# Moving the next weights' transposes, the segment sums and the leaf lookups within one block of a Mamba-style mixer, and multiplying the B C product by dt on VectorE

## The reference

```
proj = h @ in_proj_w.T            # gate z, then x B C, then dt
xBC  = silu(causal_conv4(xBC))    # 4 taps along the 32 tokens
dt   = softplus(dt + dt_bias);  dA = exp(dt * A)
state = state * dA + dt * x * B;  y = state . C      # 32 steps
y = y + x * D;  y = group_rmsnorm(y) * norm_weight * silu(z)
x = x + y @ out_proj_w
```

## Time and profile before

| | us |
|---|---|
| median of 3 runs (lowest, highest) | 3438.72 (3436.22, 3439.60) |
| the profiled execution: its time / its span | 3441.43 / 3439.3 |
| busy in the span: PE, DVE, ACT, POOL | 3311.1, 2740.2, 1746.8, 716.8 |
| granted TensorE clock, share of full speed | 0.996 |
| one iteration, groups 0 to 6 | 47.7 |
| stage 2, from its first to its last inverse root on POOL | 161 to 3160 |

### The profile page before, as it was taken

The page is one execution under the profiler, slowest core; times in us unless marked ns, Lnnn a source line. Parts: engine busy times, 40 slices in busy tenths (PEclk is TensorE's granted clock), DMA queues, the critical chain, the costliest instruction groups (busy, mean ns, idle before and its releaser), DMA issues. The chain is left out here.

```text
span 3439.3 us, 86265 instructions
## 1 busy us (share of the span) xinstructions
PE 3311.1 (96%) x33306; PEld 2741.3 (80%) x33306; DVE 2740.2 (80%) x4367; ACT 1746.8 (51%) x3203; POOL 716.8 (21%) x520
## 2 busy tenths in 40 slices
PE   8999999999999999999999999999999999999999
PEld 6777877778777787777877778777787777787888
DVE  6788888888888888888888888888888878887443
ACT  5666665555455554555555555545555555554111
POOL 1122212122221222112221122211122112221333
PEclk9999999999999999999999999999999999999999
DMA  7432363334533353335433262334423342224331
GB/s 267 168 120 106 113 232 123 116 122 161 168 124 114 125 192 134 128 110 184 133 134 133 105 220 98 134 132 176 149 98 134 140 166 98 73 98 152 93 91 58
DMA packets 207792, 466.28 MB, mean 136 GB/s; under 512 B 35134, under 2 KB 80606, under 8 KB 198284
## 3 DMA queue, kind: packets, MB, share of 16 engines
q1 hardware_dynamic: 206364, 464.72, 38.9%
q0 software_dynamic: 368, 0.85, 0.1%
q10 hardware_dynamic: 1024, 0.27, 0.0%
HBM read 313.68 MB, written 152.09 MB: 135 GB/s over the span
## 5 line engine op out<-in xcount | busy, mean ns | idle before, releaser
L1155 PE MATMUL low_banks<-ht,wt 128*128 128x512 f32 x6912 | 1612.8, 391 | 0.8 <-DVE xc L1383 0.8
L1155 PEld LDWEIGHTS low_banks<-ht,wt 128*128 128x128 f32 x6912 | 1292.4, 188 | 274.8 <-DVE xc L1383 1.2
L1383 DVE SCALAR_TENSOR_TENSOR xc<-low_banks,cvw,xc 128x496 f32<-128x496 f32 (+2 forms) x1152 | 824.9, 717 | 102.3 <-ACT xc L1287 65.9
L1243 PE MATMUL bank<-wot,gy 128*128 128x512 f32 x3072 | 733.6, 394 | 96.2 <-DVE gy L1432 96.2
L1243 PEld LDWEIGHTS bank<-wot,gy 128*128 128x128 f32 x3072 | 567.1, 188 | 236.6 <-DVE gy L1432 122.3
L1287 ACT ACTIVATE xc<-low_banks,cvb,cvw 128x512 f32<-128x512 f32 x384 | 299.8, 781 | 698.7 <-PE low_banks L1155 698.7
L1092 POOL TENSOR_TENSOR r<-rv,neg_half 128x4 f32<-128x4 f32 x64 | 64.5, 1008 | 1569.1 <-DVE rv L1465 1569.1
L1277 ACT ACTIVATE gy<-z 128x512 fp32r<-128x512 f32 x256 | 161.7, 632 | 311.1 <-DVE z L1449 311.1
L1073 POOL TENSOR_TENSOR segr<-adts,mask_le 128x1024 fp32r<-128x1024 f32 x128 | 242.8, 1918 | 336.7 <-DVE adts L1374 336.7
L1087 POOL TENSOR_TENSOR y<-y,step_of 128x512 f32<-128x512 f32 x128 | 174.8, 1389 | 627.1 <-ACT y L1293 627.1
L1473 DVE SCALAR_TENSOR_TENSOR acc<-bank,r,acc 128x512 f32<-128x512 f32 x256 | 176.7, 745 | 86.7 <-PE bank L1243 69.3
(11 more groups left out here) (195 smaller groups left out, 3726.3 us busy)
## 6 DMA issues: line engine op xcount, KB each, us to landing
ht<-h_d SPq DMA_DIRECT2D x63, 2048.0 KB, 8.6
acc_d<-acc SPq DMA_DIRECT2D x64, 1024.0 KB, 4.3
wt_d<-wnext SPq DMA_DIRECT2D x112, 512.0 KB, 3.6
acc<-acc_d SPq DMA_DIRECT2D x56, 1024.0 KB, 7.0
wt<-wt_d SPq DMA_DIRECT2D x70, 512.0 KB, 7.7
stage<-in_L_attn_in_proj_w SPq DMA_DIRECT2D x84, 256.0 KB, 2.7
wot<-wt_d SPq DMA_DIRECT2D x28, 512.0 KB, 6.3
xb<-in_x SPq DMA_DIRECT2D x8, 1024.0 KB, 7.7
```

The lines of the kernel that those rows point to most:

```text
L1155: ins = pe.matmul(pb[:, :], wt[:, n, l, k, :], ht[:, rr, k, :], start=(q == 0 and k == 0), stop=(q == 2 and k == KC - 1))
L1243: ins = pe.matmul(bank[OUT[t]][:, :], gy[:, c, l, t * P:(t + 1) * P], wot[:, rr, c, :], start=(c == 0 and q == 0), stop=(c == CT - 1 and q ...
L1383: ins = dve.scalar_tensor_tensor(dst, src, cvw[:, n, TAPS - 1 - k:TAPS - k], dst, ALU.mult, ALU.add)
```

## The change

1. **PE.** The segment sums move from behind chunk 5 and the B C products to behind chunk 3. The B C products move behind chunk 7. The transposes of the next weights move from before the scan to between the scan and chunk 9. The output projection no longer waits for both low halves at its start: its bank order becomes (7, 5, 6, 4), and ahead of banks 5 and 6 it waits for the first and the second low half.
2. **ACT.** The two `Exp` come before the tap of chunk 4. The high halves of the next weights come behind all four `skip`, one before `high(0)`, one behind it; the squares become operations of their own.
3. **DVE.** The four `pair` and `find_here` move behind the last convolution chunk. `m` is made in other steps: `joint`, the B C products spread over the heads times `step_of` (one of 128x1024), then `joint` times `decay` (two of 128x512). The last joins move behind the sums of squares; the low halves of the next weights move between the steps of the gated output.
4. **POOL.** `decay_products` is gone.

The core of the diff:

```diff
-    XT, SEG, CB, OUT, SSQ, NEXT = (4, 5, 6, 7), (4, 5), 3, (5, 6, 7, 4), 3, (5, 6)
+    XT, SEG, CB, OUT, SSQ, NEXT = (4, 5, 6, 7), (4, 5), 3, (7, 5, 6, 4), 3, (5, 6)
...
-        def decay_products(g, j):
...
-                pool.tensor_tensor(decay[:, tiles, :, :], decay[:, tiles, :, :], step_of[:, tiles, :, :], ALU.mult).then_inc(s_stepped, 1)
...
                 project(n)
+                if n == NCV - 3:
+                    sum_segments()
+
+            for c in range(CT - 2):
+                pe.wait_ge(s_conv, NCV * it + 4 + c)
+                project(NCV + c)
...
-            for u in range(2 if prepare else 0):
-                pe.wait_ge(s_raw[u], 16 * it + 16)
-                pe.wait_ge(s_dtx, TT * it + 2 + u)
-                for k in range(KC):
-                    ins = pe.transpose(bank[NEXT[u]][:, k * P:(k + 1) * P], stage[u][:, k * P:(k + 1) * P], sh.ident[:, :])
-                ins.then_inc(s_nps, 1)
             pe.wait_ge(s_m, SEGB * it + 2 * SEGB)
...
             for c in range(CT):
                 ins = scan(c)
             ins.then_inc(s_yp, 1)
+
+            for u in range(2 if prepare else 0):
+                pe.wait_ge(s_raw[u], 16 * it + 16)
+                for k in range(KC):
+                    ins = pe.transpose(bank[NEXT[u]][:, k * P:(k + 1) * P], stage[u][:, k * P:(k + 1) * P], sh.ident[:, :])
+                ins.then_inc(s_nps, 1)
+
             project(NCV + CT - 1)
 
-            if prepare:
-                pe.wait_ge(s_nlo, 2 * it + 2)
...
+                    elif c == 0 and prepare and OUT[t] in NEXT:
+                        pe.wait_ge(s_nlo, 2 * it + NEXT.index(OUT[t]) + 1)
...
+            dve.wait_ge(s_cb, it + 1)
+            dve.wait_ge(s_step, it + 1)
+            products = bank[CB][:, 0:TT * L].rearrange("p (t l) -> p t l", t=TT)
+            dve.tensor_tensor(joint[:, :, :, :], products.unsqueeze(2).to_broadcast([P, TT, HG, L]), step_of[:, :, :, :],
+                              ALU.mult).then_inc(s_stepped, 1)
```

More of the change, by code:

```diff
@@ L1174, in scan, with sum_segments @@
                 return ins
+            def sum_segments():
+                pe.wait_ge(s_segr, 2 * it + 4)
+                pe.wait_ge(s_acc, TT * it + TT)
+                for q in range(SEGB):
+                    for half in range(2):
+                        ins = pe.matmul(bank[SEG[q]][:, :], sh.mask_gtr[:, :],
+                                        segr[:, half, q * 2 * HG:(q + 1) * 2 * HG, :].rearrange("p h l -> p (h l)"),
+                                        start=(half == 0), stop=(half == 1))
+                    ins.then_inc(s_seg, 1)
             pe.wait_ge(s_ht, 16 * it + 16)
@@ L1193, in attend @@
             ins.then_inc(s_cb, 1)
[L1195 to L1205, removed]
             pe.wait_ge(s_silu, NCV * it + NCV)
@@ L1277, in high, with square, tap @@
                 act.activation(gy[:, c, 0, :], z[:, c, :], ACT.Copy).then_inc(s_uhi, 1)
+            def square(c):
                 act.activation(y[:, c, :], y[:, c, :], ACT.Square).then_inc(s_sq, 1)
-            act.activation(warm[:, :], sh.ones[:, 0:1], ACT.Silu)
-            for n in range(NCV):
+            def tap(n):
                 act.wait_ge(s_proj, NPJ * it + n + 1)
@@ L1288, in attend, with next_high @@
                                scale=cvw[:, n, TAPS - 1:TAPS]).then_inc(s_tap, 1)
-                if 0 < n < NCV - 1:
-                    silu(n - 1)
+            def next_high(u):
+                if prepare:
+                    act.wait_ge(s_nps, 2 * it + u + 1)
+                    act.wait_ge(s_nst, 32 * it + 32)
+                    act.activation(wnext[:, u, 0, :], bank[NEXT[u]][:, :], ACT.Copy).then_inc(s_nhi, 1)
+            act.activation(warm[:, :], sh.ones[:, 0:1], ACT.Silu)
+            tap(0)
+            for n in range(1, NCV - 2):
+                tap(n)
+                silu(n - 1)
             for q in range(SEGB):
@@ L1294, in attend @@
                                bank[SEG[q]][:, :], ACT.Exp).then_inc(s_exp, 1)
+            tap(NCV - 2)
+            silu(NCV - 3)
+            tap(NCV - 1)
             silu(NCV - 2)
@@ L1305, in attend @@
             gate(2)
[L1307 to L1310, removed]
             skip(2)
             skip(3)
+            next_high(0)
             high(0)
+            next_high(1)
+            square(0)
             high(1)
+            square(1)
             gate(3)
             high(2)
+            square(2)
             high(3)
+            square(3)
             act.wait_ge(s_sqturn, it + 1)
@@ L1436, in by_residue, with add_skip @@
                 return plane.rearrange("p (t b l) -> p b t l", t=TT, l=L)
[L1438 to L1442 removed]
+            def add_skip(c):
+                dve.wait_ge(s_yp, it + 1)
                 dve.wait_ge(s_skip, CT * it + c + 1)
@@ L1458, in add_squares @@
                 dve.tensor_tensor(y[:, 0, :], y[:, 0, :], y[:, c, :], ALU.add).then_inc(s_sqsum, 1)
+            dve.wait_ge(s_dnp, 16 * NDP * g + 16 * NDP)
+            add_skip(0)
+            gated(0)
+            add_skip(1)
+            low(0)
+            next_low(0)
+            gated(1)
+            next_low(1)
+            add_skip(2)
+            low(1)
+            gated(2)
             add_squares(1)
-            low(CT - 1)
+            add_skip(3)
+            low(2)
+            gated(3)
             add_squares(2)
+            low(3)
             add_squares(3)
+            join(1, lc, ld, 13)
+            join(2, lb, lc, 14)
             dve.wait_ge(s_ssq, it + 1)
             dve.tensor_scalar(rv[:, :], ssum[:, :], 1.0 / GI, EPS, ALU.mult, ALU.add).then_inc(s_rv, 1)
+            join(3, la, lb, 15)
+            w8_step(16)
+            dve.sem_inc(s_w8go, 1)
+            dve.copy_predicated(sh.w8[:, wt_tile, :], here[:, :], la).then_inc(s_w8, 1)
             dve.wait_ge(s_r, it + 1)
```

56 lines of the change are left out of this document (16 added, 40 removed).

## The result

The changed kernel takes **3421.69 us** (median of 4 runs, 3415.66 to 3422.83) against 3438.90 for the kernel before (4 runs, 3436.22 to 3439.60): ratio 0.9947, 95% interval 0.9932 to 0.9963. It is faster by 17 us, where 40 were forecast. The profiled execution took 3422.83 us, span 3421.0, granted clock 0.997.

A forecast was written before the change was run, and what follows sets the result against it. PE, busy 96% of the span, was taken as the bound, with its wait ahead of the output to gain. 41−3+3, less 1 for the tail, gave 40 us off: 3401.4 profiled, 3399 at the median; range 3384 to 3433.

The forecast's parts named there:

- segment sums, Exp, B C products: Ahead of the scan: PE does the same matmuls in another order, with no wait to shorten, so 0 gained.
- leaves 0.5 each: DVE ahead of the scan: four lookups, `find_here` and `joint` leave `m` ready with 1.8 us to spare, costing nothing.
- scan waits 0.69 for gate 8: PE at the scan: the wait for chunk 8's gate is bare; the moved transposes cost 0.83 us behind the scan.
- y plus skip S+0.11: Behind PE's end of scan (S): first low half at S+3.04, output at S+3.55, the old 1.65 us wait gone.
- new wait of 0.45 for `gate(3)`: PE in the output: bank 4 waits 0.45 us, as ACT does `high(1)` and its squares before that gate.
- next iteration S+15.5: PE's next start, at 1544.36 instead of 1545.09: 0.73 us gained in each of 56 iterations, 41 us.
- stores S+5.1, ht S+6.05: SP's queue: stores and then ht are issued behind the next weights' second low half, which ends at S+4.92.
- ht lands at S+15.6: Load of ht behind the stores: lands 0.06 us late in 55 iterations, −3 us, using up 4.2 us of slack.
- last group 0.34 × 8: Last group, 8 iterations: output 0.67 us earlier, then bank 4 waits 0.33 for `gate(3)`, a gain of 3 us.
- SP's queue: SP's later wait holds up two 512 KB stores and then the ht load; cost put at 3 us in all.
- rival 1: ht lands wholly behind the stores, at S+16.2: only 0.1 us gained in 56 iterations, 3430 us; 15%.
- rival 2: ht becomes the bound and takes longer, landing at S+17.3: 1.0 us later than before, 3494 us, slower; 6%.

The follow-up runs named there:

- run 1: The changed kernel with SP's load of ht issued ahead of the wait for the next weights and of the two stores: 3401.70 us.
- run 3: The changed kernel with ht issued ahead of the wait and the stores, and group 0's x loads also ahead of the stores: 3391.66 us.
- run 4: The kernel before, with only SP's wait ahead of the stores and ht made later, for the gated output's second low half: 3529.38 us.
- run 10: The changed kernel with ht and group 0's x loads before the stores, `gate(3)` before the squares, first next chunk transposed before the scan, halved during it: 3338.54 us.
- run 6: The changed kernel with POOL's product of decay and dt back and `m` again made from it in two operations: 3420.34 us.
- run 5: The kernel before with part 4 alone, POOL's product gone and `joint` made on DVE, nothing moved: 3408.52 us.

## Why the prediction was half right

| step, as forecast | measured |
|---|---|
| segment sums, Exp, B C products: 0 | 0; PE waits nowhere between its first projection and the scan |
| leaves 0.5 each, `find_here` 0.5 to 1.5, `joint` 1.3, `m` ready 1.8 us ahead of the scan | 0.50, 0.48, 1.22; ready at 1520.0, 2.6 us ahead of the scan |
| scan waits 0.69 for gate 8, transposes bare behind it | 0.69; 0.85 |
| y plus skip S+0.11, first low half S+3.04, output S+3.55 | S+0.17, S+3.10, S+3.71 |
| new wait of 0.45 for `gate(3)`, free at S+6.1 | S+6.04; its removal gave 0.41 |
| next iteration S+15.5 if ht is in time: gain 0.73 | S+15.54: gain 0.80 |
| stores S+5.1, ht S+6.05 | S+5.13, S+6.15 |
| **ht lands at S+15.6: 0.06 late, −3 us in all** | **mean period of groups 1 to 6 0.46 above the best; 20 us by run 1, 30 us with group 0's x loads (run 3)** |
| last group 0.34 × 8 | 0.37 |

The chain was right: with SP's order mended (run 3) the changed kernel gains 47 us, where 41 + 3 − 1 = 43 were summed without the ht term. The step that failed is **SP's queue**, the term of −3 us, in whose place runs 1 and 3 measured −30. It failed in three ways.

First, the landing of ht was one number, set against a due time 0.1 us away. The median landing was even right: 6.15 + 9.4 gives S+15.55. But lateness counts on one side only. Landings spread from 8.7 to 10.7; the early ones give nothing back, and the late ones cost up to 1.5 us. The rivals had the same mechanism, but as one fixed landing, S+16.2 (rival 1, 0.7 late) or S+17.3 (rival 2, 1.8 late); what came is a spread whose mean cost, 0.46 of a period, lies between the forecast and rival 1. Run 4 shows what 1.7 us more delay does. That landings spread could be read before. The forecast took only medians from the trace of the kernel before, where all the landings of ht were

```profile
DMA to landing us min/median/max: 7.8/8.6/9.4
```

The bounds rested on durations of other situations. Neither of the two DMA rows of before has ht right behind the stores. Of the rule of the Trainium skill cited in the prediction (DMA: Bandwidth & Descriptors, section Queues, rings and completion order), that each DMA engine consumes a queue's descriptors in ring order, the runs show the direction: behind ht (run 10) a store of 512 KB takes 9.4 us to land, ahead of it 3.3. They do not show that one transfer waits for all of the other: ht takes 9.1 us with the stores issued behind it (run 1) and 7.9 in the last group, which stores no weights. The DMA issues of the page of run 10, whose last column is the median us to landing:

```profile
ht<-h_d SPq DMA_DIRECT2D x63, 2048.0 KB, 9.2
...
wt_d<-wnext SPq DMA_DIRECT2D x112, 512.0 KB, 9.4
```

The serial sum, 11.1 us behind the first store, was too long for the median, which is 1.02 + 9.4 = 10.4 us, but not for the longest, 11.7.

Second, the prediction let PE start at the landing. The traces have 0.22 us between the two, a term that it put at nothing. With the median landing, S+15.56 in these 47 iterations, every time, PE would start at S+15.78, 0.24 late; the mean start, S+15.95, is 0.41 late. So 0.24 of the lateness is the landing and this delay, and 0.17 the spread. The last 0.05 of the 0.46 lies behind the start: from there to the next S it is 31.32 us where ht was in time and about 31.40 where it was late.

Third, group 0 was taken like groups 1 to 6. What stands behind ht in SP's queue there, the loads of x, was never costed. Its lateness reaches PE through ACT and the first convolution, which no row of before showed as a wait. By this and by ht, group 0 lost all of its gain and 2 us more.

POOL's part was right in the prediction that it changes nothing here, and the reason is run 6's. The rule of the Trainium skill on the shared pair of ports (SBUF — State Buffer, section SBUF: two separate sides), as the prediction cites it, agrees with the traces: a leaf lookup went from 1.40 us beside POOL's product to 0.50, and `find_here` from 1.52 to 0.48. What the prediction didn't draw from it is that in the old order it alone was worth 30 us (run 5).

Open: what makes one landing 8.7 us and the next 10.7 with the same issues ahead of it was not tried. Nor was it tried whether the remaining 0.25 ahead of the scan can be had.

## What to carry to other kernels

When a wait is moved on a queue, add up everything queued behind it in every kind of iteration. Compare with each due time the longest landing rather than the median, since lateness isn't averaged out by the early ones, and add the time from landing to start (0.22 us here). Put the load that the critical engine waits for ahead of stores that nobody waits for; that edit of SP's order turned 17 us into 47. And try the parts of a change alone, since two of them may remove the same stall: here one part without the others gained more than all four together.

## What the runs showed of the hardware

- SP's issue of the ht load takes 0.65 us right behind two stores. It takes 0.33 in run 1, where no store is ahead of it, and in the kernel before, where the first store is issued 1.76 us ahead. The load of ht in the changed kernel and in run 1:

```profile
L985 SPq DMA_DIRECT2D ht<-h_d x63: 332/650/790, 151.2 to 3085.1; - x63
```
```profile
L985 SPq DMA_DIRECT2D ht<-h_d x63: 326/332/339, 148.5 to 3064.8; - x63
```

- The same 2 MB land in 7.9 us where no weights are stored. In groups 1 to 6 they take 9.1 (8.5 to 9.9) with stores issued 1.2 us **behind** them (run 1), 9.4 (8.7 to 10.7) right behind the stores in the changed kernel, and 8.7 (8.1 to 9.4) in the kernel before, 1.8 us behind the first store.
- PE's first matmul starts 0.22 us behind the landing of the load that it waited for (0.21 to 0.22 in run 4, 0.21 to 0.26 in the changed kernel).
- POOL's inverse root of 128x4 elements takes 1.53 us in the changed kernel, where one of DVE's joins has begun just ahead of it (0.03 us as a rule), and took 1.01 before, where none ran beside it. In 7 iterations of the changed kernel the join begins 0.07 us behind the root instead, and the root takes 1.01 there too. So in these rows what counts is which of the two starts first. The root in the changed kernel:

```profile
L1084 POOL TENSOR_TENSOR r<-rv,neg_half x64: 1007/1534/1545, 160.4 to 3142.2; 128x4 f32<-128x4 f32 x64
```
